# Inverse transposes at the head of each large burst instead of at its end, in a fused GroupNorm and attention kernel

## The reference, cut to what matters

```python
# x: (16, 32, 32, 512) -> (16, 1024, 512), float32
h = group_norm(xf, norm_scale, norm_bias)          # 32 groups of 16 channels, eps 1e-6
qkv = h @ qkv_w + qkv_b                            # 512 -> 1536
q, k, v = split(qkv, 3)                            # each (16, 1024, 512)
q = (q * 64 ** -0.25).reshape(16 * 8, 1024, 64)    # a plain reshape: a "head" is 128 tokens
k = (k * 64 ** -0.25).reshape(16 * 8, 1024, 64)    # of all 512 channels, read as 1024 rows of 64
v = v.reshape(16 * 8, 1024, 64)
weight = softmax(einsum('btc,bsc->bts', q, k))
a = einsum('bts,bsc->btc', weight, v).reshape(16, 1024, 512)
out = xf + a @ proj_w + proj_b
```

## Time and profile before

| | us |
|---|---|
| median of 3 runs | 3664.22 (3663.39 to 3666.87) |
| the profiled execution | 3661.95 |
| its span, first to last instruction | 3660.2 |
| TensorE busy | 3439.0 (94%) |
| VectorE busy | 2790.4 (76%) |
| ScalarE busy | 2061.7 (56%) |
| GpSimd busy | 1610.8 (44%) |
| mean granted TensorE clock | 0.992 |

### The profile page before, as it was taken

The page is one execution under the profiler, slowest core; times in us unless marked ns, Lnnn a source line. Parts: engine busy times, 40 slices in busy tenths (PEclk is TensorE's granted clock), DMA queues, the critical chain, the costliest instruction groups (busy, mean ns, idle before and its releaser), DMA issues.

```text
span 3660.2 us, 67790 instructions
## 1 busy us (share of the span) xinstructions
PE 3439.0 (94%) x24640; PEld 2560.2 (70%) x24640; DVE 2790.4 (76%) x3473; ACT 2061.7 (56%) x3985; POOL 1610.8 (44%) x2762
## 2 busy tenths in 40 slices
PE   5999999999999999999999999999999999999998
PEld 4767777676676767767677677777777767676775
DVE  4778778787787787877777777777778778787776
ACT  4555555565655655556555555655555555555553
POOL 3444444444444444444444444444444444444442
PEclk9999999999999999999999999999999999999999
DMA  3768777677776777767777777777768777677777
GB/s 111 178 164 191 177 176 184 162 194 176 170 193 165 191 171 181 190 166 183 177 180 179 175 186 171 184 177 171 193 162 192 182 176 187 165 191 169 173 183 171
DMA packets 255707, 646.87 MB, mean 177 GB/s; under 512 B 73872, under 2 KB 73872, under 8 KB 255376
## 3 DMA queue, kind: packets, MB, share of 16 engines
q1 hardware_dynamic: 235792, 604.79, 69.7%
q10 hardware_dynamic: 19584, 37.76, 2.9%
HBM read 71.84 MB, written 33.55 MB: 29 GB/s over the span
## 4 chain that ended last, share of the span: by engine, by line
PE 72%; ACT 13%; DVE 6%; POOL 4%; issue 4%; SPq 1%; DMA 0%; POOLq 0%; ACTq 0%; DVEq 0%
PE s_ps L344 16%; PE pv_ps L373 16%; PE c_ps L407 8%; PE c_ps L408 6%; PE c_ps L409 6%; ACT staged L495 6%; ACT probs L475 6%; PE c_ps L419 4%; PE c_ps L421 3%; PE c_ps L420 3%; DVE turned L608 3%; PE c_ps L391 2%; PE c_ps L392 2%; PE c_ps L393 2%; DVE neg_max L625 2%
## 5 line engine op out<-in xcount | busy, mean ns | idle before, releaser
L475 ACT ACTIVATE probs<-s_ps,neg_max 128x1024 f32<-128x1024 f32 x1024 | 1140.6, 1114 | 856.4 <-DVE neg_max L625 854.8
L625 DVE TENSOR_REDUCE neg_max<-s_ps 128x1 f32<-128x1024 f32 x1024 | 1202.8, 1216 | 470.9 <-PE s_ps L344 470.8
L608 DVE STREAM_TRANSPOSE turned<-probs 128x1024 f32<-128x1024 f32 x1024 | 1225.7, 1226 | 297.4 <-ACT probs L475 263.6
L373 PE MATMUL pv_ps<-probs_t,v 128*64 128x256 f32 x8192 | 944.2, 383 | 6.6 <-DMA probs_t<-turned 6.6
L779 POOL COPY inv_wide<-inv_sum 128x256 f32<-128x256 f32 x256 | 101.5, 397 | 1896.1 <-PE pv_ps L355 1888.8
L373 PEld LDWEIGHTS pv_ps<-probs_t,v 128*64 128x64 f32 x8192 | 568.8, 137 | 358.1 <-issue 95.9
L495 ACT ACTIVATE staged<-c_ps,qk_bias 64x256 f32<-64x256 f32 x1024 | 479.3, 468 | 356.1 <-POOL kl L756 254.1
L407 PE MATMUL c_ps<-h_hi,w_hi 128*128 128x256 f32 x2048 | 626.1, 306 | 43.6 <-ACT staged L495 21.5
L409 PE MATMUL c_ps<-h_hi,w_lo 128*128 128x256 f32 x2048 | 586.5, 286 | 0.0
L408 PE MATMUL c_ps<-h_lo,w_hi 128*128 128x256 f32 x2048 | 586.2, 286 | 0.0
L407 PEld LDWEIGHTS c_ps<-h_hi,w_hi 128*128 128x128 f32 x2048 | 397.5, 194 | 144.1 <-issue 77.6
(11 more groups left out here) (71 smaller groups left out, 4877.3 us busy)
## 6 DMA issues: line engine op xcount, KB each, us to landing
probs_t<-turned SPq DMA_DIRECT2D x4096, 128.0 KB, 2.4
x_res<-in_x SPq DMA_DIRECT2D x128, 256.0 KB, 3.0
result<-x_res ACTq DMA_DIRECT2D x128, 256.0 KB, 3.1
x_next<-in_x SPq DMA_DIRECT2D x120, 256.0 KB, 3.4
probs_t<-in_L_conv_qkv_w ACTq DMA_DIRECT2D x4, 768.0 KB, 8.8
turned<-in_x SPq DMA_DIRECT2D x4, 512.0 KB, 12.8
probs_t<-in_L_conv_proj_w ACTq DMA_DIRECT2D x4, 256.0 KB, 13.8
v_bias<-in_L_conv_qkv_b SPq DMA_DIRECT2D x1, 256.0 KB, 16.9
```

The source lines that it names most:

```text
L373: last = nc.tensor.matmul(pv_ps[side][CH * par:CH * (par + 1), 0, :], v_sb[:, ring_of(i, parity), CH * chunk:CH * (chunk + 1)], p_t[:, par ...
L475: nc.scalar.activation(probs[k % 2][:, :], s_ps[k % 2][:, :], ACT.Exp, bias=neg_max[:, k % 4:k % 4 + 1], accum_out=row_sum[:, (k // HALF) ...
L608: nc.vector.transpose(dst, probs[k % 2][:, :].rearrange("p (k b j) -> p k b j", k=CHUNKS, b=QUADS)).then_inc(probs_turned, 1)
L625: nc.vector.tensor_reduce(neg_max[:, k % 4:k % 4 + 1], s_ps[k % 2][:, :], AX.X, ALU.max, negate=True).then_inc(max_ready, 1)
```

## The change

The call of `spread_inverse` moves from behind the loop over the burst's units to ahead of it. It stays behind the two scores of the step. The order of the units (burst 4 with its q product ahead of the projection) is the same in both kernels.

```diff
                 if k % HALF == 0:
+                    if within(s - SPREAD_LAG, N_SLOTS):
+                        spread_inverse(b, k)
                     for i, (kind, n) in enumerate(LARGE[k % 16]):
                         if i == SMALL_BEFORE:
                             small(b, k)
                         make[kind](b, k, i, n)
-                    if within(s - SPREAD_LAG, N_SLOTS):
-                        spread_inverse(b, k)
```

## The result

The changed kernel takes 3438.93 us in the median of three runs (3436.25 to 3439.35), against 3664.22 before. The ratio is 0.9383, 95% interval 0.9365 to 0.9402.

What follows compares the result with a forecast made beforehand. TensorE's own work plus handovers making it late, chiefly work queued behind GpSimd's copy, bound the kernel. Gains 162 (burst 8) + 32 (k=48) + 1 (last batch) = 195 gave 3467, or 3469 against the runs' median; range 3445 to 3530.

Steps and rivals of the forecast that it cites:

- The chain of burst 8: GpSimd's copy waits for the end transposes, delaying split, staging, exps and score bank; whole excess goes, gain 162 us.
- the shifted schedule: Burst 8 re-timed with transposes at its head: exps run 1837.6 to 1839.9, TensorE wants banks at 1840.6 and 1841.4.
- The own cost of burst 12: Burst 12 without waits, read from burst 4: 13.47 with a statistics transpose, 13.0 without.
- The transposes' price at the two places: Two transposes per half cost TensorE 0.31 wherever they stand, at the burst's head or end.
- The group step: Burst 12 at k=44: 13.4 after the change, with 0.2 left of a bank wait of 1.10.
- the slower rival: Transposes at the head hold the whole burst when the widened copy is late: 3750, chance 0.04; forecast costs this wait 0.
- Half stays: Rival: ScalarE still comes late to burst 8's exps, half of the 162 gain is lost: 3550, chance 0.09.
- nothing happens: Rival: staging wait is a symptom, exps are late for another reason, the maximum: 3664, chance 0.04.
- Splits beside VectorE: Rival: GpSimd's splits before staging products 4 and 5 each lose a VectorE transpose, 1.23: 3500, chance 0.05; forecast adds nothing.
- Clock: Low clock after burst 8's wait, in 7 statistics and 2 group intervals, expected to go; 11 us of the 162.
- Moves: A half's 16 DMAs take up to 13.9 us of SyncE's queue; costed at 0 though half-periods shrink to 13.3.
- VectorE's cover of 0.42: Products and v end 0.31 later, covered by VectorE's 0.42 wait for scores after second v; without cover, 20 us.

Runs made afterwards that it cites:

- the two-buffer kernel: Kernel before with transposes still at the burst's end, but inv_wide given a second buffer (projection's bias row left out, v's bias added instead): 3462.27 us, ratio 0.9433.
- the head in burst 8 alone: Against the kernel before, transposes moved to the head in burst 8 only, left at the end in bursts 0, 4 and 12: 3488.49 us, ratio 0.9505.

## Why the prediction was right in kind and short in size

*The chain of burst 8: right.* Copy, split, staging, exp and score bank are released in this order, shown by the two-buffer kernel and by the head in burst 8 alone. The exps of the shifted schedule were to free the banks 1.5 to 1.9 before they are wanted; the first ends at 1777.54, 1.5 before the scores at 1779.06. The marks 8 to 12 (L355, now at the heads) read 13.31 and 12.88, forecast 13.5 and 13.0.

*The own cost of burst 12: the step that failed.* "Burst 12 has the same instructions as burst 4 ... So its own cost is 13.47" was wrong, and with it the terms 30 x 13.47 and 15 x 13.0 of the sum, as burst 4 itself waited 0.23 to 0.26 for its q staging. The own cost is 13.24 at the end and 13.17 with the transposes at the head; without statistics 12.80 and 12.74, where I had 13.0. Over the three plain bursts 12 of a batch that is 0.3 each, 0.9: about 0.65 from the reference that held a wait, and 0.2 from the head's place.

*The same wait in burst 4: a gain that was not in the sum.* I had seen that the transposes now stand ahead of the wait and are covered by it, but only for the bursts without statistics. It holds in all: 13.50 to 13.28, 0.22 in three intervals, 0.6 a batch. In the last pair of the batch (k=52) I predicted 13.17 and it was 13.27, which takes 0.1 back.

*The transposes' price at the two places: not equal.* I held "0.31 wherever they stand". In the intervals without the wait of burst 4 (the two-buffer kernel with the end against the changed one) the head saves 0.03 at burst 0, 0.09 at burst 8 and 0.07 at burst 12. That is about 0.6 more than predicted in a batch at bursts 8 and 12, part of which is in the 13.17 above, and 0.1 at burst 0.

*The group step: over-estimated.* At k=44 I left 0.2 of the bank wait of 1.10; 0.43 is left, which takes some 0.3 back.

Together: the forecast's own intervals make 12.69 x 3 + 13.60, 13.47 x 3 + 13.17, 13.41 x 3 + 12.94 and 13.47 x 2 + 13.4 + 13.0, which is 211.8 a batch. (13.60 is the interval of the marks from k=44 to k=48 in the kernel before. The prediction gave 12.69 for all of its kind and left this one as it was.) Measured are 210.17. The difference of 1.6 is 0.9 at burst 12, 0.5 at burst 4, 0.4 at burst 8 and 0.15 at burst 0, less 0.25 that the group step takes back. 1.6 x 15 is 24 of the 28 us that the spans differ from the forecast; the other 4 lie in the first batch and the last.

*The head's wait for the copy (the slower rival): did not come.* With one buffer and with two the time is the same, and the copy of a half ends one burst before it is needed (1768.19 for the head at 1780.64).

*Half stays, nothing happens: fell.* TensorE's wait for exp is 5.6.

*Splits beside VectorE: not seen.* The row of the subtraction in the changed kernel, for the earlier trace rows:

```profile
L756 POOL TENSOR_TENSOR kl<-staged,kh x256: 722/739/743, 49.6 to 3361.5; 128x256 fp32r<-128x256 f32 x128
```

The median went from 731 to 739 ns, and the longest from 738 to 743, so the prediction's own sign of being wrong, "L756 over 0.74", is met by 3 ns. Its premise, that the splits had run in VectorE's idle time, does not hold: by start and duration, 252 of the 256 overlap a VectorE instruction in both kernels. Before, all 252 ran beside the maxima (L625), 63 of them also beside a transpose; in the changed kernel 144 run beside the transposes (L608, median 741), 45 beside the statistics alone (L683, 739) and 63 beside the maxima (738). A lock for a whole VectorE instruction, which the Trainium skill (SBUF — State Buffer, Who interferes with whom) describes for two-port modes and two SBUF inputs, would have shown as 1.2 us; no such wait shows at the operations that meet here.

*Clock: right in sum, the count misread.* No stretch at the low clock is left in the middle of the changed kernel. In the kernel before there are eleven, each right after the wait of a burst 8: seven in intervals of burst 12 with statistics, which took 1.5 longer (some 10 us in all, where I had 11), and four at k=44, in batches 4, 6, 11 and 13, whose intervals are 16.10 like their neighbours. The two group intervals of 17.23 that I had put down to the clock by their length are long for another reason: they are batches 2 and 6, where the interval of the burst 8 ahead is 15.46 and not 15.19, and batch 2 has no low-clock stretch there. The changed kernel has no such intervals.

*Moves, and VectorE's cover of 0.42: right.* TensorE waits for the moves twice, as before, and the wait for the scores after the second v is 0.21.

*The range.* It took in slips that cost and hardly any that bring: 3445 left 24 for the gains I had missed, and they were 30. The term with the most uncertain size, the own cost of a burst, had only a bound from above, since all rows that it was read from could hold waits.

## What to carry to other kernels

A producer-consumer buffer with one slot holds not only its writer but all that is queued behind the writer in program order. Look for the engine that "waits for nothing that matters" and read what its next instructions are and who waits for those; then release it by moving the reader up, or by a second buffer.

A stage is a clean reference for another only if its weight loads show no wait. Read the waits of PEld beside those of PE before you call an interval the engine's own work, and take the shortest like interval as one end of the range.

## What the runs showed of the hardware that was not expected

Two transposes between scores and a product cost less than between a product and scores. By the starts of TensorE's matmuls (medians, for a burst that begins and ends with 128x256 products): at the head there are 0.32 from the last scores to the first transpose, 0.17 to the second and 0.03 to the product, in place of 0.32 from scores straight to a product, so the two add 0.19. At the end there are 0.12, 0.11 and 0.20, in place of 0.21 from a product straight to scores, so they add 0.22. That makes 0.04. The intervals differ by 0.03 at burst 0, 0.07 at burst 12 and 0.09 at burst 8; what the last two have above 0.04 is not accounted for.

The release of GpSimd's copy hardly depends on the place. The copy starts 0.57 after the first transpose's start at the head, 0.52 at the end and 0.52 between products (medians). At three places of the program (k=40 of batch 2, k=4 of batch 5, k=8 of batch 8) it starts 0.29 later, in the kernel before and in the changed one alike; the burst of the changed kernel shown above is one of them (0.86, 1767.33 to 1768.19). What these places have in common was not tried.
